# A decoder layer on one core: products of weights and values in halves of 1024 columns, exponentials written key by head

## The reference

```python
x = _layernorm(x + _L0_attn_ref(x, Wq, Wk, Wv, Wo, bo))
x = _layernorm(x + _L0_xattn_ref(x, ctx_1024, ctx_1024))
x = _layernorm(x + _L0_ffn_ref(x, gate, experts_w1, experts_w2, experts_w3))
```

```python
att = softmax(einsum('nqhd,nkhd->nhqk', q, k) / sqrt(hd))
out = einsum('nhqk,nkhd->nqhd', att, v)
```

## Time and profile before

| | before |
|---|---|
| three runs | 944.56, 949.15, 949.77 us |
| the profiled execution's own time | 951.18 us |
| its span in the trace | 949.3 us |
| busy: PE, PEld, DVE, ACT, POOL | 776.7, 591.8, 768.1, 631.0, 579.4 us |
| mean granted TensorE clock | 0.915 of full speed |
| L1561 POOL products | 256 instructions, 293.0 us busy, mean 1179 ns |
| L1577 POOL scatters | 128 instructions, 127.5 us busy, mean 996 ns |

### The profile page before, as it was taken

How to read it: one execution, slowest core, us unless ns; L and a number is a source line. 1 busy time by engine, 2 the same in 40 slices (tenths; PEclk the granted TensorE clock), 3 DMA queues, 4 the chain that set the end, 5 groups by cost and what they waited for, 6 DMA issues and landing times. The chain is left out here.

```text
span 949.3 us, 34272 instructions
## 1 busy us (share of the span) xinstructions
PE 776.7 (82%) x11844; PEld 591.8 (62%) x11844; DVE 768.1 (81%) x2039; ACT 631.0 (66%) x1544; POOL 579.4 (61%) x567
## 2 busy tenths in 40 slices
PE   2577789999999999999777627999999999999400
PEld 2356556656666666666544316999999999999400
DVE  5888887999999999999876555888888888888465
ACT  1334456888888888788779735676767667676255
POOL 0366774699999999999974470444444444444353
PEclk9777899999999999999979857999999999999755
DMA  8511221222232222222222041222222222221276
GB/s 224 176 19 32 38 42 32 40 64 57 52 67 67 48 61 66 51 54 58 51 48 59 29 93 49 66 62 63 63 61 64 61 66 61 64 64 52 87 246 228
DMA packets 136741, 68.49 MB, mean 72 GB/s; under 512 B 74528, under 2 KB 125984, under 8 KB 136576
## 3 DMA queue, kind: packets, MB, share of 16 engines
q1 hardware_dynamic: 121440, 40.56, 18.6%
q0 software_dynamic: 8640, 17.84, 5.8%
q10 hardware_dynamic: 6496, 7.89, 2.6%
HBM read 37.91 MB, written 28.34 MB: 70 GB/s over the span
## 5 line engine op out<-in xcount | busy, mean ns | idle before, releaser
L1561 POOL TENSOR_TENSOR prod_ev<-e_sb,q_v 128x512 f32<-128x512 f32 x256 | 293.0, 1179 | 82.6 <-ACT e_sb L871 60.1
L1602 POOL DMA_INDIRECT token_halves<-w_new,tok_i x142 | 135.9, 957 | 190.2 <-DVE w_new L1504 168.3
L1577 POOL DMA_INDIRECT routed_rows<-xe,pos x128 | 127.5, 996 | 64.5 <-DVE pos L1341 31.0
L1171 DVE TENSOR_TENSOR prod_qk<-q_v,QKV 128x2048 f32<-128x2048 f32 x64 | 145.6, 2276 | 3.5 <-PE SC L572 2.2
L1488 DVE TENSOR_TENSOR prod_ev<-prod_qk,prod_ev 128x1024 f16<-128x1024 f32 x71 | 87.0, 1226 | 56.1 <-ACT prod_ev L1051 56.1
L1051 ACT CAST prod_ev<-prod_qk 128x1024 f16<-128x1024 f32 x71 | 74.2, 1045 | 72.4 <-DVE prod_qk L1514 58.6
L780 PE MATMUL QKV<-k_t,w_hl 128*128 128x256 f16 x852 | 117.5, 275 | 0.0
L780 PE MATMUL ST<-k_t,w_hl 128*128 128x256 f16 x852 | 117.0, 274 | 0.0
L1060 ACT ACTIVATE prod_qk<-QKV,silu_scale 128x512 f32<-128x512 f32 x142 | 96.1, 678 | 12.5 <-PE QKV L780 10.3
L1514 DVE SCALAR_TENSOR_TENSOR prod_qk<-ST,hid_scale,prod_qk 128x512 f32<-128x512 f32 x142 | 99.5, 742 | 2.7 <-ACT prod_qk L1060 2.7
L932 ACT ACTIVATE q<-XT,tab 128x256 f32<-128x256 f32 x256 | 96.0, 476 | 5.9 <-PE XT L637 5.8
(11 more groups left out here) (168 smaller groups left out, 1551.4 us busy)
## 6 DMA issues: line engine op xcount, KB each, us to landing
w_new<-routed_rows SPq DMA_DIRECT2D x71, 130.0 KB, 2.2
prod_ev<-token_halves SPq DMA_DIRECT2D x16, 512.0 KB, 4.9
x_sb<-x SPq DMA_DIRECT2D x128, 32.0 KB
head_rows<-o_n SPq DMA_DIRECT2D x128, 32.0 KB
o_t<-head_rows SPq DMA_DIRECT2D x64, 64.0 KB, 2.7
ctx_sb<-ctx SPq DMA_DIRECT2D x32, 128.0 KB, 2.8
out<-prod_qk ACTq DMA_DIRECT2D x16, 256.0 KB, 3.9
token_halves<-w_new,tok_i POOLq DMA_INDIRECT x142, 2.2
```

The source lines that it names most:

```text
L1171: eng.tensor_tensor(prod_qk[:, u, :, :].rearrange("p d (i j) -> p d i j", j=NH), q.unsqueeze(3).to_broadcast([P, HD, NH, NH]), k.unsqueeze ...
L1561: ins = eng.tensor_tensor(prod_ev[:, u, q, :, :, 0:HD], e_sb[:, it.slot(2), u, 64 * q:64 * q + 64].rearrange("p (i j) -> p j i", j=4).unsq ...
L1577: eng.indirect_dma_start(out=xs, out_offset=bass.IndirectOffsetOnAxis(ap=pos[:, r, 2 * u + k:2 * u + k + 1], axis=0), in_=xe[:, r, u, k, : ...
L1602: eng.indirect_dma_start(out=halves, out_offset=bass.IndirectOffsetOnAxis(ap=tok_i[:, s, u:u + 1], axis=0), in_=yw[:, s, u, :], in_offset= ...
```

## The change

POOL's 8 instructions of 512 columns for each duo become 4 of 1024, one for each u and half (quarters 0 and 1, or 2 and 3). To let one access pattern run over two quarters, ACT writes the exponentials as (u, q, j, i), key by head, instead of (u, q, i, j). The numbers computed are the same. ACT reads `SC` in the old order and writes with a step of 16 elements (64 bytes) from one key to the next; POOL reads the exponentials without a step between heads where it had one of 4 elements (16 bytes); `beside` reads 256 elements in a row where it read in steps of 4. No wait or semaphore is changed.

```diff
             def exponent(it):
-                eng.activation(e_sb[:, it.slot(2), :, :].rearrange("p u i -> p (u i)"), SC[:, :], ACT.Exp,
-                               scale=float(HD) ** -0.5).then_inc(e_ready, 1)
+                eng.activation(e_sb[:, it.slot(2), :, :].rearrange("p u (q j i) -> p (u q) i j", q=4, j=4),
+                               SC[:, :].rearrange("p (u i j) -> p u i j", u=8, j=4), ACT.Exp, scale=float(HD) ** -0.5).then_inc(e_ready, 1)
...
             def beside(it, u):
-                eng.copy(prod_ev[:, u, :, :, :, HD], e_sb[:, it.slot(2), u, :].rearrange("p (q i j) -> p q j i", q=4, j=4)
+                eng.copy(prod_ev[:, u, :, :, :, HD], e_sb[:, it.slot(2), u, :].rearrange("p (q j i) -> p q j i", q=4, j=4)
                          ).then_inc(beside_ready[u], 1)
...
             def weighted(it, u, half):
-                for q in range(2 * half, 2 * half + 2):
-                    ins = eng.tensor_tensor(
-                        prod_ev[:, u, q, :, :, 0:HD],
-                        e_sb[:, it.slot(2), u, 64 * q:64 * q + 64].rearrange("p (i j) -> p j i", j=4).unsqueeze(3).to_broadcast([P, 4, NH, HD]),
-                        q_v[:, it.slot(RING), u, 1, QUARTER * q:QUARTER * q + QUARTER].rearrange("p (j d) -> p j d", d=HD).unsqueeze(2).to_broadcast([P, 4, NH, HD]),
-                        ALU.mult)
+                n = slice(8 * half, 8 * half + 8)
+                ins = eng.tensor_tensor(
+                    prod_ev[:, u, :, :, :, 0:HD].rearrange("p q j i d -> p (q j) i d")[:, n, :, :],
+                    e_sb[:, it.slot(2), u, :].rearrange("p (n i) -> p n i", i=NH)[:, n, :].unsqueeze(3).to_broadcast([P, 8, NH, HD]),
+                    q_v[:, it.slot(RING), u, 1, :].rearrange("p (n d) -> p n d", d=HD)[:, n, :].unsqueeze(2).to_broadcast([P, 8, NH, HD]),
+                    ALU.mult)
```

## The result

Four runs of the changed kernel gave 931.58, 933.04, 934.44 and 937.76 us, median 933.7, against 949.5 for the kernel before (four runs): a ratio of 0.985, 95% interval 0.981 to 0.989. The profiled execution took 931.6 us (span 929.8) against 951.2 (949.3).

A forecast was written before the change was run, and what follows sets the result against it. Stage A's end was taken to bound the kernel, at POOL's 14.24 us pace from 427 us. Lag 1.3, four bursts 0.8 and last burst 0.2 gave 2.3 us off 949.15: 946.9 us, range 941.5 to 953.

The forecast's parts named there:

- POOL's lag: Stage A: POOL's bursts, 14.13 us apart against steps of 14.06, start ever later behind ACT's exponential; 1.3 us to regain.
- the ring through SP: Stage A: DVE's `o_n`, SP's store and load, PE's projection, next `o_n`; loads of new x, 2.30 us, stand inside it.
- until 416 us the step is set by none of them: Stage A: no engine's busy time sets the 14.06 us step before 416 us; direct gain there nothing.
- POOL's saving for a duo: POOL's burst of products: 4 fewer instructions save 0.20 us, between 0 and 0.61, so 9.03 us becomes 8.83.
- The fixed part of an instruction: POOL's products: the cost that doesn't grow with columns, 0.03 us by the memsets, upper bound 0.153.
- POOL gets much faster: Rival, chance 0.14: without the 16-byte jump in reading exponentials, POOL's burst shrinks by whole microseconds; `posw` 7.9 us earlier, 941.3 us.
- let go 2.3 us earlier with all behind it: End of stage A: `posw`, stalled by POOL's last burst, and everything behind it come 2.3 us earlier, otherwise untouched.
- the slow write: ACT's exponential, written in 64-byte steps: 0.3 us more, between 0 and 0.58, hidden by 0.8 us of cover; cost 0.
- The order between DVE and POOL: Stage A: DVE's `xq_b` starts 0.11 us before the exponential's end, so POOL's burst doesn't catch it; cost 0.
- Nothing fixed: Rival, chance 0.14: POOL's instructions have no fixed cost, so the burst stays 9.03 us; time 949 us.
- slower by ACT: Rival, chance 0.07: ACT's scattered exponential write takes 1.1 us more, costing 0.3 us in some 25 steps; 954.4 us.
- slower by POOL: Rival, chance 0.06: a 1024-column product costs 0.1 us more than two of 512, 0.4 a duo; 958 us.

The follow-up runs named there:

- d1_padded: e1_quarters plus one extra POOL product of 384 columns for each duo, into a tile nobody reads: 947.0 us, ratio 0.9997 to the kernel before.
- s2_after_sp: The changed kernel with SP's loads of `o_t` put ahead of its loads of new x and context: 918.6 us, ratio 0.969.
- e1_quarters: The changed kernel with POOL's products issued again as 8 instructions of 512 columns for each duo: 935.2 us, ratio 0.984.
- e2_slow_write: The kernel before with only ACT's new scattered write of the exponentials, weights permuted among heads and keys: 945.2 us, ratio 0.9955.
- s1_before_sp: The kernel before with SP's loads of `o_t` put ahead of its loads of new x and context: 939.5 us, ratio 0.9915.
- d3_padded_less: e1_quarters plus one extra POOL product of 128 columns for each duo, into a tile of its own: 936.6 us, ratio 0.989.
- e3_fast_write: The changed kernel with ACT's exponentials written in a row again, weights permuted among heads and keys: 933.1 us.
- b1_permuted: The changed kernel with PE writing the scores key by head into PSUM, so that ACT writes in a row: 935.1 us.

## Why the prediction was wrong, point by point

**What bounds the kernel: right, and incomplete.** POOL's lag, DVE's product of two SBUF tiles waiting for POOL, and the ring through SP are all shown: by d1_padded, which brings the stalls back, and by s2_after_sp. That the product doesn't get through while POOL's products follow one another is too strong: it holds in every stall of the kernel before, but in four profiles (both of the changed kernel, s2_after_sp, e1_quarters) `posw` gets through at the end of a product in the middle of the last burst. And "until 416 us the step is set by none of them" was read off one execution; in the second one POOL sets the pace from 372 us. Steps 8 to 27 lose 3.1 us with the change, and the prediction had put nothing there. What these 3.1 us are stays open: the first profile of before has no stalled `posw` in that stretch and still takes 266.9 us, and e1_quarters, with a short burst and no stall there either, takes 268.1.

**The term that was mis-sized: POOL's saving for a duo.** Forecast 0.20 us, between 0 and 0.61; measured 1.32. Two faults. The fixed part of an instruction was put at 0.03 to 0.05 us, by the memsets; it is 0.14 us, close to the upper bound of 0.153, which came from a product of 4 columns and one of 512. The nearer row was the one of the same operation. And the sum left the pattern out: it stood among the rivals only, as something worth whole microseconds or nothing. It is 0.093 us an instruction, 0.74 for a duo. The rule of GPSIMD Engine Reference, Performance pitfalls for Q7 kernels, in the Trainium skill points the right way, but its half more for each element isn't what happens here: 1.124 against 1.031 us is 9%, with the jump taken once in 8 elements.

**The same sum with the measured term.** With 1.32 us POOL no longer binds in the last steps. The stretches from exponential 27 to `pos` shrink by 3.4 + 3.4 = 6.8 us; the rival "POOL gets much faster" had said 7.9. So the arithmetic of lag and release was right, and given the right term it would have said 941 to 942 us: still 8 us too much. Of these, 4.7 us are in the next paragraph; the 3.1 us above are the rest of what the profiles show.

**The step that was missing: TensorE's clock behind the stall.** The sum took what follows the last burst as fixed, "let go 2.3 us earlier with all behind it". It isn't. The same stretch in both kernels, from the `pos` behind the last burst on, before (columns as in the earlier trace rows; the last three are the granted clock, DMA share and GB/s):

```profile
484.70:496.30 11.60, 10.90 (x107) 5.86 (x107) 7.39 (x34) 7.43 (x21) 5.83 (x6) 0.59 0.13 38
496.30:504.60 8.30, 5.36 (x54) 2.71 (x54) 6.63 (x31) 8.23 (x29) 3.83 (x4) 0.99 0.49 113
504.60:516.00 11.40, 8.99 (x122) 5.58 (x120) 6.63 (x31) 9.13 (x31) 3.83 (x4) 0.85 0.08 26
```

and after:

```profile
470.80:479.30 8.50, 7.58 (x135) 4.59 (x127) 7.28 (x34) 7.68 (x26) 5.85 (x6) 1.00 0.38 86
479.30:488.20 8.90, 6.29 (x71) 3.57 (x75) 6.63 (x31) 8.83 (x31) 3.83 (x4) 1.00 0.49 105
488.20:497.70 9.50, 6.86 (x114) 4.04 (x104) 6.68 (x31) 9.11 (x31) 3.83 (x4) 1.00 0.10 31
```

The same work takes 31.3 us before and 26.9 after. While DVE stood in `posw` for 6 us, PE idled 3.5 us, and its clock fell to half speed for most of a step (0.59 on the mean) and again two steps on. So it is in five profiles (before, its second run, e2_slow_write, d1_padded, s1_before_sp), with stalls of 4.4 to 6.0 us: the clock is at half for 3.4 to 9.7 us of the first step behind the burst, that step takes 9.4 to 11.6 us, and the whole emptying, from `pos` to stage B, 89.3 to 92.7. In the nine others the clock is not at half there, the step takes 7.9 to 10.0 us and the emptying 85.1 to 88.1. In the means of the two kernels' profiles this is worth 4.7 us.

The nine include d3_padded_less, whose stall is 5.20 us and whose emptying takes 86.8: there a long stall without the slow clock cost nothing behind itself. So, as far as this one profile shows, the 4.7 us go with the clock and not with the stall's length. What decides whether the clock falls isn't shown. The second run of before has the shorter stall, 4.44 us, and loses it; PE's idle pieces around the last burst are 0.38 and 2.37 us there and 1.91 and 1.58 us in d3_padded_less, which keeps it.

**ACT: right, but for a size.** 0.3 us was taken for the slow write, 0.46 measured; it was said to be covered and is (e3_fast_write, b1_permuted). The rule on 16-byte lines (the Trainium skill, SBUF — State Buffer, Door 1) holds for ACT's write: 1.03 against 0.57 us. For its read it doesn't show: the copies, whose write is scattered in both kernels, read in a row now and are hardly faster, 0.664 against 0.670 us.

**The order between DVE and POOL: right.** `xq_b` isn't caught in any profile: it never takes more than 0.49 us (0.42 at the median), and the soonest that a burst starts is 0.08 us after the exponential's end.

**"Nothing fixed", "slower by ACT", "slower by POOL"** didn't happen. The range failed because its lower end, 941.5, was worked out from the most that a faster POOL could bring (941.3), with the clock and the earlier steps at nothing.

What stays open: why e2_slow_write is 4 us faster than the kernel before, why s1_before_sp gains 8 us at the median, where the 3.1 us of steps 8 to 27 come from, when `posw` gets through between two products, what decides whether the clock falls behind a stall, and what makes the first stretch vary from 142 to 150 us from one execution to another.

## What to carry to other kernels

When an engine's stall is shortened, what follows isn't only earlier: the work behind a long stall can run at half clock, as in five of six profiles here, so look at the granted clock behind the stall and add the price of the slow stretch, read from rows at both levels. An engine whose pace lies within about 1% of the others' sets the time in some executions and not in others: 0.4 us of POOL's burst was worth 10 us here and the next 1.2 us nothing, so before sizing a gain find the length at which the engine stops binding. And take an instruction's fixed cost from two sizes of the same operation, not from a simpler one.

## What the runs showed of the hardware

* POOL's product of two tiles costs 0.14 us an instruction and 1.74 ns a column when one operand is repeated 8 times and the other read in a row; with a 16-byte jump after each 8 reads 512 columns cost 0.09 us more.
* DVE's products of two SBUF tiles wait for POOL's products, often past the end of one to the end of the burst: `posw` waited 5.99 us across five such ends before the last (from 478.50 on, at a pitch of 1.124 us). But not always: in e1_quarters and in the changed kernel it got through at an end in the middle of the burst. No run shows what decides it.
* ACT's write of 4-byte values in steps of 64 bytes costs 0.46 us for 512 values, 0.9 ns each, more than in a row.
* PE's writes to PSUM in steps of 64 bytes and DVE's maximum reading PSUM so cost nothing more: L572 takes 0.379 us at the median in b1_permuted and in the changed kernel (ends of matmuls are modelled), and L1181 0.680 us in both.
* Behind a long stall of DVE TensorE's granted clock was at half for 3.4 to 9.7 us of the next step in five profiles, and at full in a sixth, with a stall of 5.20 us.
